# Linear attention and a mixture of experts on one core: attention rows stored as high and low fp16 halves, expert tiles loaded by transposing DMAs into four buffers

## What is computed

```
x = x + linear_attention(layernorm(x))      # 16 heads of 16, feature map elu + 1, causal
x = x + moe(layernorm(x))                   # 8 experts, top 2, 256 -> 512 (gelu) -> 256
# moe, for a token: probs = softmax(top-2 logits)
# out = sum over its 2 experts of probs[e] * (gelu(x @ w1[e] + b1[e]) @ w2[e] + b2[e])
```

## Time and profile before

| | us |
|---|---|
| median of 3 runs | 1096.58 |
| lowest, highest | 1094.77, 1099.1 |
| the profiled execution, device time | 1091.56 |
| its span, first to last instruction | 1089.8 |
| mean granted TensorE clock, share of full speed | 0.963 |
| busy: PE, DVE, ACT, POOL | 951.3, 831.0, 660.6, 699.4 |

### The profile page before, as it was taken

The page is one execution under the profiler, slowest core; times in us unless marked ns, Lnnn a source line. Parts: engine busy times, 40 slices in busy tenths (PEclk is TensorE's granted clock), DMA queues, the critical chain, the costliest instruction groups (busy, mean ns, idle before and its releaser), DMA issues. The chain is left out here.

```text
span 1089.8 us, 33554 instructions
## 1 busy us (share of the span) xinstructions
PE 951.3 (87%) x10092; PEld 784.3 (72%) x10093; DVE 831.0 (76%) x2201; ACT 660.6 (61%) x1253; POOL 699.4 (64%) x606
## 2 busy tenths in 40 slices
PE   4599888988898898888889833999999999999995
PEld 2377667766766775675677733999999999999994
DVE  5378999998997997997999874666666666666663
ACT  5667776776776677666767432555555555555552
POOL 5626677786677678776778553556556565566555
PEclk9799999999998999998999966999999999999998
DMA  3665886446654654673655282455555555555554
GB/s 111 149 142 125 274 178 156 126 153 161 165 126 137 159 132 135 155 173 98 164 139 139 89 316 97 89 90 96 96 96 88 87 98 96 97 85 95 92 97 49
DMA packets 129125, 140.30 MB, mean 129 GB/s; under 512 B 12512, under 2 KB 122208, under 8 KB 128416
## 3 DMA queue, kind: packets, MB, share of 16 engines
q1 hardware_dynamic: 101184, 102.38, 38.0%
q0 software_dynamic: 26688, 35.93, 17.8%
q10 hardware_dynamic: 1184, 1.18, 0.3%
HBM read 72.01 MB, written 67.44 MB: 128 GB/s over the span
## 5 line engine op out<-in xcount | busy, mean ns | idle before, releaser
L1497 POOL DMA_INDIRECT out<-yt,to_token x142 | 225.7, 1589 | 172.8 <-DVE yt L1360 108.6
L792 ACT ACTIVATE ahl<-pS 128x512 f16<-128x512 f32 x240 | 141.0, 599 | 74.7 <-PE pS L508 73.1
L1035 DVE SCALAR_TENSOR_TENSOR ahl<-pS,ahl 128x512 f16<-128x512 f32 x240 | 161.2, 682 | 28.8 <-ACT ahl L792 27.5
L1414 POOL DMA_INDIRECT expert_in<-xn,cur x128 | 130.5, 1020 | 35.1 <-issue 33.1
L960 ACT ACTIVATE g<-pS,b1s 128x256 f32<-128x256 f32 x144 | 60.2, 470 | 90.7 <-PE pS L433 90.7
L433 PE MATMUL pF<-xT,was 128*128 128x512 f16 x384 | 102.7, 410 | 11.8 <-DVE xT L1040 11.8
L505 PE MATMUL pS<-cbs 128*128 128x512 bf16 x240 | 93.0, 387 | 20.2 <-DVE ahl L1035 12.2
L1331 DVE TENSOR_TENSOR ghl<-g,ghl 128x1024 f16<-128x1024 f32 x71 | 87.1, 1227 | 24.3 <-ACT ghl L982 24.3
L433 PE MATMUL pU<-w2s,ghl 128*128 x864 | 100.5, 273 | 1.9 <-DVE ghl L1331 1.9
L433 PE MATMUL pS<-gT,w1s 128*128 128x256 f16 x864 | 101.1, 274 | 0.1
L433 PE MATMUL pF<-w2s,ghl 128*128 x840 | 97.4, 273 | 0.0
(11 more groups left out here) (160 smaller groups left out, 2323.9 us busy)
## 6 DMA issues: line engine op xcount, KB each, us to landing
xg<-expert_in SPq DMA_DIRECT2D x71, 260.0 KB, 3.0
qk_parts<-qkhl SPq DMA_DIRECT2D x32, 512.0 KB, 2.9
qst<-qk_parts SPq DMA_DIRECT2D x96, 128.0 KB
kst<-qk_parts SPq DMA_DIRECT2D x48, 256.0 KB
xs<-x SPq DMA_DIRECT2D x16, 512.0 KB, 4.6
xr<-x SPq DMA_DIRECT2D x16, 512.0 KB, 4.8
out<-x SPq DMA_DIRECT2D x16, 512.0 KB, 3.2
expert_in<-pads SPq DMA_DIRECT2D x16, 260.0 KB, 3.7
```

The costliest lines, as they stand in the source:

```text
L792: nc.scalar.activation(ahl[:, b % 2, 0, n * 4 * C:(n + 1) * 4 * C], score_bank(fr, n)[:], ACT.Relu).then_inc(sc_hi, 1)
L1035: V.scalar_tensor_tensor(ahl[:, b % 2, 1, cols], score_bank(fr, n)[:], 0.0, ahl[:, b % 2, 0, cols], ALU.max, ALU.subtract).then_inc(sc_lo, 1)
L1414: G.indirect_dma_start(xg_dram, bass.IndirectOffsetOnAxis(ap=cur[:, qp, 2 * b + t:2 * b + t + 1], axis=0), xn2[:, qp, b], None).then_inc(s ...
L1497: G.indirect_dma_start(out, bass.IndirectOffsetOnAxis(ap=to_token[:, c % 2, s:s + 1], axis=0), yt[:, c % 2, s], None, compute_op=ALU.add). ...
```

## The change

1. In attention the normalised rows are no longer stored as float32. `norm2_apply` writes them back into x1 (in place), and has to wait until SP's DMA of x1 to `out` has landed (`x1_out`). Two new ACT instructions a step (`rows_high`, 128x512 each) round x1 to fp16 into the first half of a row of `data`, and two new DVE instructions (`rows_low`, 128x512 each) write x1 minus that into the second half. A row is still 1040 bytes. The router's transposes read x1. The next step's `residual` waits for `rows_lo` in place of `x1_out` and `xn2_done`.
2. In the expert stage a tile's rows are loaded by one transposing DMA from `expert_in`, seen as 256 rows of 512 fp16 numbers, straight into gT (four 128x256 pieces: two high, two low). `turn`, the expert stage's `rows_high` and the DVE subtraction behind it are gone. The four router numbers of the rows are loaded by a second DMA (`about`, 256 pieces of 16 bytes). Both have four buffers; SP issues the load of tile t once the hidden layer of tile t-4 has ended.
3. The hardware loop of the expert stage has four tiles instead of two.

```diff
-        xn2 = sb("xn2", [P, 2, B, ROW], F32, att)
+        data = sb("data", [P, 2, B, ROW], F32, att)
...
-        xg = sb("xg", [P, 2, 2, ROW], F32, moe)
-        gT = sb("gT", [P, 2, 2, KC * MT], F16, moe)
+        about = sb("about", [P, BUFS, 2, ROW - D], F32, moe)
+        gT = sb("gT", [P, BUFS, 2, KC, MT], F16, moe)
...
+        rows = data[:].bitcast(F16)
...
+                if c >= BUFS or not isinstance(j, int):
+                    sp.wait_ge(h_ps, 2 * t - 2 * BUFS + 2)
+                    carry_wait(sp)
+                    sp.wait_ge(meta, t - BUFS + 1)
+                    carry_wait(sp)
+                sp.dma_start_transpose(gT[:, c % BUFS].rearrange("p a k n -> p (a k) n"),
+                                       xg_dram[bass.ds(row, MT), 0:D].bitcast(F16)).then_inc(gT_in[c % BUFS], 16)
+                sp.dma_start(about[:, c % BUFS],
+                             xg_dram[bass.ds(row, MT), D:ROW].rearrange("(s p) d -> p s d", p=P)).then_inc(about_in[c % BUFS], 16)
...
-                    pe.wait_ge(gt_lo, t + 2)
+                    pe.wait_ge(gT_in[p4], 16 * ((c + 1) // BUFS + 1) + 16 * j)
...
-                    for k in range(KC):
-                        for s in range(MT // P):
-                            mm = nc.tensor.transpose(rows_T[c % 2][:, k * MT + s * P:k * MT + (s + 1) * P],
-                                                     xg[:, c % 2, s, k * P:(k + 1) * P], ident)
-                    mm.then_inc(gt_ps, 1)
...
+                def rows_high(n):
+                    act.wait_ge(xn2_done, 4 * r + 2 * n + 2)
+                    if c >= 4 and n == 0:
+                        act.wait_ge(scat_out[c % 2], 128 * rh)
+                    nc.scalar.activation(rows[:, c % 2, 2 * n:2 * n + 2, 0:D], x1[:, 2 * n:2 * n + 2], ACT.Copy).then_inc(rows_hi, 1)
...
                 if ro:
+                    rows_high(0)
                     row_copy(0)
+                    rows_high(1)
...
-                    nc.scalar.activation(gT[:, c % 2, 0], rows_T[c % 2][:], ACT.Copy).then_inc(gt_hi, 1)
...
                     if b == 0:
                         dve.wait_ge(ln2_rs, r + 1)
-                        if c >= 4:
-                            dve.wait_ge(scat_out[rp], 128 * rh)
-                    V.scalar_tensor_tensor(xn2[:, rp, b, 0:D], x1[:, b], mv2[:, b, 0:1], rs2[:, b:b + 1].to_broadcast([P, D]),
+                        dve.wait_ge(x1_out, 16 * r + 16)
+                    V.scalar_tensor_tensor(x1[:, b], x1[:, b], mv2[:, b, 0:1], rs2[:, b:b + 1].to_broadcast([P, D]),
                                            ALU.subtract, ALU.mult).then_inc(xn2_done, 1)
+                def rows_low(n):
+                    dve.wait_ge(rows_hi, 2 * r + n + 1)
+                    V.scalar_tensor_tensor(rows[:, rp, 2 * n:2 * n + 2, D:2 * D], x1[:, 2 * n:2 * n + 2], 1.0,
+                                           rows[:, rp, 2 * n:2 * n + 2, 0:D], ALU.mult, ALU.subtract).then_inc(rows_lo, 1)
...
-                if is_tile(j, c + 2):
-                    dve.wait_ge(gt_hi, t + 3)
-                    V.tensor_tensor(gT[:, c % 2, 1], rows_T[c % 2][:], gT[:, c % 2, 0], ALU.subtract).then_inc(gt_lo, 1)
```

More of the change, by code:

```diff
@@ L294, in tiles @@
                 body(0, c)
-            with engine.Fori(0, (NT - 5) // 2) as j:
-                for c in (2, 3):
+            with engine.Fori(0, LOOPS) as j:
+                for c in range(2, 2 + BUFS):
                     body(j, c)
-            for c in range(2 + (NT - 5) // 2 * 2, NT):
+            for c in range(2 + LOOPS * BUFS, NT):
                 body(0, c)
@@ L403, in _ @@
             sp.wait_ge(tab, TAB)
+            sp.wait_ge(tail_out, 16 * E)
+            sp.wait_ge(pads_out, 16 * (E + 1))
+            for n in range(2):
+                sp.wait_ge(scat_out[n], 128 * STEPS // 2)
             def load(j, c):
-                t, th = front_of(j, c)
-                if not is_tile(j, c):
-                    return
+                t, _ = tile_of(j, c)
                 row = sp.value_load(table[0:1, 0, bass.ds(t, 1)], min_val=0, max_val=ROWS - MT)
[L410 to L422, removed]
+                if c >= BUFS or not isinstance(j, int):
[7 more added lines that the diff above has]
+                             xg_dram[bass.ds(row, MT), D:ROW].rearrange("(s p) d -> p s d", p=P)).then_inc(about_in[c % BUFS], 16)
+            for c in range(BUFS):
+                load(0, c)
+            with sp.Fori(0, LOOPS - 1) as j:
+                for c in range(BUFS, 2 * BUFS):
+                    load(j, c)
+            for c in range(LOOPS * BUFS, NT):
+                load(0, c)
         @block.tensor
@@ L1077, in out_lo, with residual @@
                                     ALU.subtract).then_inc(aT_lo, 1)
[L1079 removed]
+                def residual(s, b, buffer, first=False):
                     g = 4 * s + b
                     dve.wait_ge(wo_ps, g + 1)
+                    if b % 2 == 0 and not first:
+                        dve.wait_ge(rows_lo, 2 * s - 1 + b // 2)
                     if b == 0:
                         dve.wait_ge(xr_done, s + 1)
[L1084 to L1087 removed]
                     V.scalar_tensor_tensor(x1[:, b], pA[:, D:2 * D], 1.0 / WS, xr[:, buffer, b], ALU.mult, ALU.add).then_inc(x1_done, 1)
@@ L1199, in body @@
                         norm2_apply(b)
+                    rows_low(0)
+                    rows_low(1)
                 else:
@@ L1213, in body @@
                         score_lo(1, 3)
+                    if ro:
+                        rows_low(0)
                 if bk:
-                    residual(s, 0, sp_)
+                    residual(s, 0, sp_, c == 1)
                 if fr and c >= 2:
@@ L1221, in body @@
                     state_part(1)
+                if ro and c != STEPS:
+                    rows_low(1)
                 if nx:
```

77 lines of the change are left out of this document (31 added, 46 removed).

## The result

| | before | changed |
|---|---|---|
| median of the runs | 1095.67 us (1093.29 to 1099.1) | 1115.24 us (1113.84 to 1117.77) |
| ratio | | 1.0179 (1.0145 to 1.0213) |
| profiled execution | 1091.56 us, span 1089.8 us | 1115.56 us, span 1113.8 us |

The changed kernel is 1.8% slower, where the prediction had it 0.7% faster. Four marks in the two traces, in us from the start of the span, say where the 24.0 us between the two spans lie. (The medians are 19.6 us apart: the profiled execution of the kernel before lies 4.1 us under its median, that of the changed kernel on it.)

What follows compares the result with a forecast made beforehand. DVE and the key chain were taken to bound attention, PE the expert stage. Terms -31 - 1.5 + 22 + 3 = -7.5 us gave 1084 us profiled, 1089 us as median, range 1068 to 1136.

Steps and rivals of the forecast that it cites:

- 14 equal steps: Attention: 14 steps with a full body, each costed at +1.6 us on a 36.82 us step without back edge: +22 us.
- DVE in attention: Two added subtractions a step, 2.1 us, of which 0.5 us is absorbed: +1.6 us a step, +22 us over 14 steps.
- rival 2: Attention pays in full: rows_low meets POOL both times, 3.0 us a step; +14 us, 1111 us; chance 0.18.
- ACT in attention: Two added roundings, 1.3 us a step, hide on average and run beside DVE's 2.1 us; if added, 18 us more.
- The wait for x1_out: Wait moves to norm2_apply(0), mostly free in a full body, late in the drain: +3 us, between 0 and +6.
- Expert stage: Four transposes a tile leave PE, which stays the bound at 5.23 us a tile: 71 tiles, -31 us.
- rival 3: Expert stage: the transposing load makes the DMA engines the bound, from 34 engine-us a load; 1139 to 1245 us; chance 0.17.
- rival 4: Expert stage gains only half, as later adds reach PE through POOL and DVE at expert changes; 1104 us; chance 0.09.
- First tile: From the first expert load's issue to the first hidden product, 5.3 us before: -1.5 us.

Runs made afterwards that it cites:

- e17_best: Changed kernel with one small memset ahead on DVE, second rows_high behind score_hi(2, 0), and the last step's norm written to xs: 1075.48 us, 0.9838.
- e18_before_two: The kernel before with two small memsets ahead of everything on DVE: 1094.44 us, ratio 1.0005.

## Why the prediction was wrong

**What failed** is the view of attention as 14 equal steps. The prediction took a step "that holds no back edge", measured it, and never priced the edges. Of the 38.8 us that 13 steps grew, 11.3 come with the four back edges: the eight steps around them took 12.1 us more than eight steps without one before (307.1 against 8 x 36.87), and 23.4 now (335.3 against 8 x 38.98). The prediction put that term at nothing without a reason. Its signs were there before the run: q14's 40 packets, the idle time put down to issue, and the change's seven more instructions ahead of DVE's loop and ten more in it. None of the rivals had it. It is chance of place, not a property of the change: with the start at 449 in both, the ratios are 0.9942 and 0.9938, and with loops written out 0.9984 and 0.9927, while the two other changed kernels without gaps have 0.9993 and 1.0017. So the change by itself is between no difference and 0.8% slower; both pairs of traces say 0.8% (spans 1093.9 and 1085.3, 1092.8 and 1083.8). The forecast of a gain fails without the back edges too: 24.0 - 11.3 leaves 12.7 us of loss where 7.5 of gain were forecast.

**DVE in attention**, +1.6 us a step: measured 2.1. The duration was right, 0.68 + 1.37 to 1.43 against 2.1 forecast, one of the two meeting POOL; rival 2, where both do, did not come. The 0.5 us that was to be absorbed was not: DVE's idle time rose, from 2.2 to 2.9 us a step. What came off instead is 0.8 us in `w1_low` (1.50 to 0.67), because the POOL product that it used to meet now starts 0.4 us behind it (175.10 against 174.69), late by a wait of 2.8 us for ACT.

**ACT in attention** "hides": the step that was wrong in kind. It gives back that gain: DVE's waits for ACT's rounded scores rise from 0.77 to 1.46 us a step, and moving `rows_high(1)` takes 1.1 us off the step. That it stood ahead of the fourth feature tile was seen and set beside DVE's time as if the two were parallel. They are in series: `rows_high(1)` waits on ACT for DVE's norm (L846: 34.7 us in all, 26 times), the scores that ACT rounds stand behind it, and DVE's low parts wait for these. The way that had been looked at was not it: `rows_low` waited for ACT only once, 1.0 us.

**The wait for x1_out**, +3: the last two steps and the gap took 10.3. The place was right and the landing was not: the median of 3.2 us was taken for the one DMA that mattered, whose 11.5 was in the same row. `e17_best` gives 4.8 us for it. Of the other 5.5, 4.3 lie in the last two steps, which differ by more than that between traces of like kernels, and 1.2 in the gap; their cause stays open.

**Expert stage**, -31: measured -23.3. PE stayed the bound and the beat fell to 5.24, as forecast, and neither rival 3 nor rival 4 came. At 10.48 for every pair of tiles it would be 35 x 0.87 = -30.5 up to the 71st tile; it is -26.2, because the first pair takes 11.44 (10.60 before) and others 10.55 to 10.95. The first hidden tile took 5.21 us at a granted clock of 0.52 (nearly all at the lower level, 1.2 GHz) against 3.67 at 0.75 before. That the transposes just ahead of it had raised the clock before is not shown: with the same transposes it took 5.30 us at 0.51 in `e18_before_two`. From the 71st tile to the end it takes 2.8 us more. Over the whole stage DVE now waits 93.7 us for the adds to land (`yt` of line 1359; 2.4 before), and POOL 62.0 (37.4 before); PE does not see it, but the adds are what is late next. The term was mis-sized by 7.7 us.

```profile
719.06 5.21 PE L452 MATMUL pS<-gT,w1s 128*128 128x256 f16 x24 [21.42 <-DMA gT<-expert_in]
```

**First tile**, -1.5: measured -1.9.

In sum: 16.8 of the 31.5 us between forecast and trace in the body steps (11.3 back edges, the rest ACT in series and a slack that was not there), 7.3 in the last steps and the drain, 7.7 in the expert stage, -0.4 at the first tile.

## What to carry to other kernels

Before an edit to a program with a hardware loop, count the instructions from the engine's start to the loop and in it: bodies of 305 and 315 were free of fetches at the back edge only from some starts, and one instruction was worth 2%. Look at the "instruction" queues of the profile and at idle time put down to issue; when comparing two versions, place both loops alike, or the place is what is measured. A wait on a DMA is priced by the queue in front of that very DMA, and an instruction on a second engine is in series with the busiest one if it waits for it and stands ahead of what it waits for, however idle its engine is on average.

## What the runs showed of the hardware

- One small memset ahead of the loop moved a 1.1 ms kernel by 24 us; the idle time appears in no semaphore wait, only as issue, and in packets of an instruction queue (40 against 20), five packets of 8.2 KB a back edge.
- A transposing DMA of 256 rows of 1024 bytes ran as packets of 256 bytes at 20 ns each in the mean, where the plain load of the same rows took 67 ns for packets of 1 KB; together with the small load, whose packets of 16 bytes took 10.5 ns, it cost 23.4 engine-us a tile. Its issue on SP takes 1.26 us, that of a plain load 0.4.
- A DVE instruction with two SBUF inputs of 128x512 took 0.68 us alone and 1.37 to 1.43 in the same place of each step beside POOL, and edits elsewhere changed the duration of its neighbours (`w1_low`, 1.50 to 0.67). A tiny one pays as much: `pd` of 128x4 (line 1119 before) took 0.15 us in the last steps and 1.7 to 2.0 in the others; at 184.42 it lasts 1.92 us, to the end of a POOL operation that had begun at 183.94 and takes 2.36.
